# Attention: both transposes of a group's first two units before its value product

## What is computed

```
B, S, D = 8, 512, 512; N_HEAD = 16; HEAD_DIM = 32
q = (x @ Wq + bq), k = (x @ Wk + bk), v = (x @ Wv + bv)      # split in 16 heads of 32
scores = einsum('bhqd,bhkd->bhqk', q / sqrt(HEAD_DIM), k) + attention_bias
scores = where(src_mask, -inf, scores)
probs  = softmax(scores, axis=-1)
ctx    = einsum('bhqk,bhkd->bhqd', probs, v)
x      = x + (ctx @ Wo + bo)
```

## Time and profile before

| | |
|---|---|
| median of 3 executions | 2872.56 us (2868.95 to 2876.88) |
| the profiled execution | 2875.56 us, its span 2873.8 us |
| TensorE busy in the span | 2659.9 us, 93% |
| VectorE, GpSimd, ScalarE busy | 1771.7 us (62%), 1026.4 us (36%), 951.0 us (33%) |
| attention, steady part | 280 to 1195 us |
| transposes of probabilities, L1021 | 2048, 313.6 us busy |

### The profile page before, as it was taken

How to read it: one execution, slowest core, us unless ns; L and a number is a source line. 1 busy time by engine, 2 the same in 40 slices (tenths; PEclk the granted TensorE clock), 3 DMA queues, 4 the chain that set the end, 5 groups by cost and what they waited for, 6 DMA issues and landing times. The chain is left out here.

```text
span 2873.8 us, 48156 instructions
## 1 busy us (share of the span) xinstructions
PE 2659.9 (93%) x17072; PEld 2040.2 (71%) x17088; DVE 1771.7 (62%) x3500; ACT 951.0 (33%) x2032; POOL 1026.4 (36%) x741
## 2 busy tenths in 40 slices
PE   6975999999999999699999999996999999999997
PEld 2434777777777777477888888885777777777775
DVE  8965777777777777565444444433665665566544
ACT  1114666666666666311111111111112111211212
POOL 1004787777777775531111001102332222222210
PEclk9997999999999999899999999998999999999998
DMA  4325554554545545331100000001543343233311
GB/s 156 113 82 168 166 188 144 184 170 162 189 144 183 191 140 164 114 103 45 30 1 31 30 31 1 30 15 61 165 121 103 99 120 108 93 116 117 98 46 37
DMA packets 212640, 306.13 MB, mean 107 GB/s; under 512 B 14266, under 2 KB 93178, under 8 KB 209722
## 3 DMA queue, kind: packets, MB, share of 16 engines
q1 hardware_dynamic: 210682, 299.88, 32.3%
q0 software_dynamic: 1728, 3.16, 0.5%
HBM read 268.94 MB, written 34.05 MB: 105 GB/s over the span
## 5 line engine op out<-in xcount | busy, mean ns | idle before, releaser
L783 POOL TENSOR_TENSOR at_bias<-at_bias,at_mask 128x1024 f32<-128x1024 f32 x224 | 480.0, 2147 | 248.0 <-DMA at_bias<-in_fside_Bx16xSxS 246.7
L1148 DVE CUSTOM_DVE_ANT_0 at_bias<-at_bias,at_bank_score 128x512 f32<-128x512 f32 x512 | 337.7, 680 | 183.2 <-PE at_bank_score L1014 137.8
L875 ACT ACTIVATE at_y<-at_bias,at_nmax 128x512 f32<-128x512 f32 x512 | 366.5, 717 | 20.3 <-DVE at_nmax L1148 20.3
L1542 POOL TENSOR_SCALAR expert_WH<-expert_stage 128x1024 fp32r<-128x1024 f32 x128 | 164.3, 1284 | 516.4 <-PE expert_bank_out L98 315.9
L1021 PE MATMUL at_bank_probT<-at_ident,at_y 128*128 128x128 f32 x2048 | 313.6, 280 | 6.6 <-ACT at_y L875 6.6
L1876 DVE CAST ff_gH<-ff_g 128x512 fp32r<-128x512 f32 x128 | 70.0, 547 | 387.1 <-ACT ff_g L1615 386.8
L1021 PEld LDWEIGHTS at_bank_probT<-at_ident,at_y 128*128 128x128 f32 x2048 | 228.6, 141 | 94.7 <-issue 66.2
L1615 ACT ACTIVATE expert_g<-expert_bank_hid,expert_b1c 128x512 f32<-128x512 f32 x128 | 88.3, 690 | 623.7 <-PE expert_bank_hid L98 623.7
L1615 ACT ACTIVATE ff_g<-ff_bank_hid,ff_b1c 128x512 f32<-128x512 f32 x128 | 88.2, 689 | 610.1 <-PE ff_bank_hid L98 610.1
L883 ACT ACTIVATE at_probT<-at_bank_probT 128x512 f32<-128x512 f32 x256 | 153.0, 598 | 272.0 <-PE at_bank_probT L1021 159.7
L1876 DVE CAST expert_gH<-expert_g 128x512 fp32r<-128x512 f32 x128 | 68.5, 535 | 259.7 <-ACT expert_g L1615 259.7
(11 more groups left out here) (327 smaller groups left out, 5657.8 us busy)
## 6 DMA issues: line engine op xcount, KB each, us to landing
at_bias<-in_fside_Bx16xSxS SPq DMA_DIRECT2D x256, 512.0 KB, 3.5
expert_stage<-in_L_cond_Wi SPq DMA_DIRECT2D x128, 256.0 KB, 2.9
expert_stage<-in_L_cond_Wo SPq DMA_DIRECT2D x128, 256.0 KB, 3.0
st_f<-in_x SPq DMA_DIRECT2D x8, 1024.0 KB, 7.0
x_after_layer<-st_y SPq DMA_DIRECT2D x8, 1024.0 KB, 4.8
at_x<-x_after_layer SPq DMA_DIRECT2D x32, 256.0 KB, 4.6
x_after_attention<-at_x SPq DMA_DIRECT2D x32, 256.0 KB, 2.3
ff_x<-x_after_attention SPq DMA_DIRECT2D x32, 256.0 KB, 4.0
```

Source lines behind the costliest of these rows:

```text
L783: pool.tensor_tensor(bias[i % NB][:, :, :], bias[i % NB][:, :, :], mask[:, i // 2 % R, :].unsqueeze(1).to_broadcast([P, 2, S]), ALU.add).t ...
L875: act.activation(prob[u % 2][:, :], bias[u // 2 % NB][:, u % 2, :], ACT.Exp, scale=-1.0, bias=nmax[:, u % 4:u % 4 + 1], accum_out=sums[:, ...
L1148: dve.tensor_tensor_reduce(t, t, pS[u % HC][:, :], -1.0, 3.0e38, ALU.add, ALU.min, nmax[:, u % 4:u % 4 + 1]).then_inc(s_max, 1)
L1542: pool.tensor_scalar(WH[:, f, :], stage[f % 2][:, :], 1.0, 0.0, ALU.mult, ALU.add).then_inc(s_wh, 1)
```

## The change

In TensorE's loop over the units, the transposes of the second unit of a group (u mod 4 = 1) no longer stand at their own place, behind the value product of u mod 4 = 0, but directly behind the first unit's, in front of the value product. The waits go with them. The third and fourth units' transposes stay. No other engine's code is touched.

```
@@ -1069,8 +1069,10 @@
                         if nxt and u in (42, 46, 50):
                             pe.wait_ge(s_xl, (n + 1) * C + {42: 1, 46: 3, 50: 4}[u])
                         scores(n, (u + 2) // HC)
-                    if cur:
+                    if cur and u % HC != 1:
                         transpose_probs(n, u)
+                    if cur and u % HC == 0:
+                        transpose_probs(n, u + 1)
                     if u % HC == 0 and (prev or u > 4) and (cur or u <= 4):
                         values(n, u, cur)
                     if it == 2 and cur and (prev or c > 0):
```

## The result

The changed kernel takes **2926.76 us** (median of 4, 2923.69 to 2928.83) against 2874.72 before (median of 4): a ratio of **1.0188, 95% interval 1.0176 to 1.0200**, some 54 us more by the ratio. The forecast was 2929 in 2904 to 2948. The profiled execution has a span of 2924.5 us where it was 2873.8: 50.7 more.

The account below looks back on a forecast made before the run. TensorE was taken to set attention's pace. Terms 34.0 + 2.8 + 6.7 + 3.7 + 7.3 + 2 = 56.5 us took the profiled 2875.56 to 2932, a median of 2929 us; range 2904 to 2948.

Parts of the forecast that it names:

- The return path: Value product through ScalarE's even copy, exponential and context copy to next scores: 2.81 us, no longer hidden; 0.27 a group, 34.0 us.
- P directly behind V: Projections straight after the value product on TensorE: any gain or larger gap lies inside the 2.81 us path, not counted.
- The faster rival: Projections need no gap after the value product, scores don't wait for the context copy: 0.20 a group, 2847 us; chance 0.04.
- T1's wait for exp(u1): Second unit's transposes, now before the value product, wait for their exponential: 0 to 0.28 us ordinarily, more at u = 28, 32.
- u = 48: Value product at u = 0 mod 16: second transposes wait for their exponential, 0.28 us; 6.7 us over 24 groups.
- The five groups without projections: One in first batch, four at end, TensorE already idle: about 2 us over the 0.27 each, an estimate.
- u = 24: Value product at u = 8 mod 16: exponential there in time, no wait, so only the 0.27 us.
- u = 28: In 7 batches second transposes wait for an exponential ending late: 0.52 us over the 0.27, 3.7 us in all.
- u = 32: In 7 batches ScalarE has no gap, the exponential comes 0.39 later: 1.04 us each, 7.3 us in all.
- The return path alone (2907): Rival: exponentials come early enough everywhere, so only the longer path to the scores costs, 34 us; chance 0.08.
- ScalarE falling behind everywhere: Rival: no ScalarE gap after the context copy, some 94 groups wait 0.17 more, 16 us on top, 2945 us; chance 0.08.
- No change: Rival: the value product would have been waiting anyway for VectorE's sums of the scores, 2873 us; chance 0.06.

Follow-up runs that it names:

- The two edits that shorten the path: Changed kernel with ScalarE's context copy ahead of the next exponential: 2896.07 us, ratio 1.0070; changed kernel with three buffers of transposed probabilities: 2894.18 us, ratio 1.0059.
- the run with u = 24 alone: Kernel before, with the two units' transposes paired only in the group whose value product stands at u = 24 (8 groups): 2872.18 us, one execution.

## Why the prediction was right

The time, its sign and its mechanism came out; two terms of the sum did not. The distance between successive value products, after less before, was worked out from the starts of L1037 in both traces (means of the first seven batches; the last batch has other groups). A distance holds the cost of a late V and the gain of the 0.17 us by which S now follows V sooner.

| V at u | predicted | measured |
|---|---|---|
| 8, 12, 40, 44, 56, 60 | 0.27 | 0.26 to 0.33 |
| 0, 16, 48 | 0.55 | 0.53, 0.56, 0.26 |
| 4, 20, 36, 52 | 0.36 | 0.36 to 0.39 |
| 24 | 0.27 | 1.19 |
| 28 | 1.27 | -0.12 (0.52 in the first batch) |
| 32 | 0.84 | 0.74 |

**The return path: right in each number.** V after T0 0.97, S after V 2.82 (2.81), even copy at V + 1.21, 0.14 from the context copy to S. The term was 34.0 us. The two edits that shorten the path should leave 0.03 a group, so take away 30. In the traces they take 28 and 33 us off the time from the first to the last value product of attention; by the ratios it is 34 and 37, with some 7 us of uncertainty each.

**P directly behind V: right to leave out.** No row showed it. It keeps the gap of 0.20 that T1 had: V to P is 1.01. The faster rival had needed it to vanish.

**T1's wait for exp(u1): right but for u = 48.** At u = 0, 4, 16, 20, 36 and 52 as worked out, to 0.03. At u = 12 and 60 it isn't zero but 0.04: the read comes some hundredths late. At u = 48 of the full batches it is zero, not 0.28, which is 2 us less: four transposes of the next batch's rows (L960, 0.44 us) stand ahead of T0 there and give the exponential time. The five groups without projections cost some 2 us in all over the 0.27 each, as estimated.

**u = 24: the step that failed.** The prediction let T1 wait for the exponential alone, and put u = 24 with u = 8 at nothing. In seven groups, those of u = 24 in every batch but the last, it waits for the bank (and once more, for 0.2 us, in the last batch):

```profile
676.73 0.68 DVE L1109 BATCH_NORM_STATS2 at_stats<-at_x 128x6 f32<-128x512 f32 x1
676.81 0.60 PE L1021 MATMUL at_bank_probT<-at_ident,at_y 128*128 128x128 f32 x4
676.88 0.18 ACT L875 ACTIVATION_READ_ACCUMULATOR at_y<-at_bias,at_nmax 128x1 f32 x1
...
677.34 0.67 DVE L1157 COPY at_probT<-at_bank_probT 128x512 f32<-128x512 f32 x1
...
678.16 0.63 PE L1021 MATMUL at_bank_probT<-at_ident,at_y 128*128 128x128 f32 x4 [0.74 <-DVE at_probT L1157]
```

exp(u1) is over at 677.06, but the odd copy of u = 23 starts only at 677.34, behind VectorE's row statistics, and T1 waits 0.74 us until it has freed bank pT[1]. T1 in front of V has two waits, and where VectorE carries the statistics the second one comes last. In the kernel before V's 1.01 us covered it. It cost 0.93 us in 7 batches, 6.5 us.

**u = 28: the second mis-sized term.** The forecast took over the kernel before's VectorE, where the subtraction L1116 takes 1.76 us and exp(u1) is late by that. After, its time is

```profile
683.71 0.17 DVE L1118 TENSOR_SCALAR at_mneg<-at_mv 128x4 f32<-128x4 f32 x1
```

0.17 us. GpSimd's mask addition in the two kernels, first before, then after:

```profile
894.12 2.15 POOL L783 TENSOR_TENSOR at_bias<-at_bias,at_mask 128x1024 f32<-128x1024 f32 x1
```

```profile
681.13 2.14 POOL L783 TENSOR_TENSOR at_bias<-at_bias,at_mask 128x1024 f32<-128x1024 f32 x1
```

Before, 894.12 + 2.15 = 896.27 and the subtraction ends at 896.29; after, 681.13 + 2.14 = 683.27, 0.44 before it starts. The group is later by then, the mask addition is out of the way, and 1.4 us a batch come back against the forecast: 10 us. The prediction had named this row as its uncertainty but put it at 6 us either way.

**u = 32: right.** TensorE's timeline of u = 20 to 32:

```profile
915.88 1.08 PE L1037 MATMUL at_bank_score<-at_probT,at_v 128*32 128x128 f32 x32
...
924.25 1.08 PE L1037 MATMUL at_bank_score<-at_probT,at_v 128*32 128x128 f32 x32
...
931.62 1.08 PE L1037 MATMUL at_bank_score<-at_probT,at_v 128*32 128x128 f32 x32
...
937.74 0.60 PE L1021 MATMUL at_bank_probT<-at_ident,at_y 128*128 128x128 f32 x4
939.05 0.66 PE L1021 MATMUL at_bank_probT<-at_ident,at_y 128*128 128x128 f32 x4 [0.71 <-ACT at_y L875]
939.64 1.08 PE L1037 MATMUL at_bank_score<-at_probT,at_v 128*32 128x128 f32 x32
```

T1 starts 1.31 behind T0 (1.42 forecast) and V 0.59 behind that.

The sum: 56.5, plus 6.5 for u = 24, less 10 for u = 28 and 2 for u = 48, is 51; 50.7 in the span and 52 between the medians were measured. The two failed terms have opposite signs, and that the total is closer than its parts is luck. In the kernel they are tied: the run with u = 24 alone shows that the delay there is what moves the subtraction out from under the mask addition, and the run with the statistics moved, which takes the first wait away, gets nothing for it.

**The rivals.** The return path alone (2907) falls: with the path cut the kernel still loses 17 to 20 us. ScalarE falling behind everywhere falls: the classes at u = 4 and 8 are as forecast. No change and faster fall with the result.

**What the profile was to show.** The wait before the scores, the even copy's larger wait, V to S of 2.82 and T0 to V of 0.97 came. Two readings were put wrongly: the wait for L891 is named in 55 places and not in over 100, since most are too short to be given a releaser, and stands as 22.7 us of idle time in the row of L1014; and TensorE's busy time in attention did not stay but rose from 898.97 to 920.38 us, though its instructions are the same. Matmuls' ends are modelled and overlap, so that part of the lost time is booked as busy: in the group above the last projection's record ends at 736.99, and only 0.15 of the 0.22 us is booked as idle.

## What to carry to other kernels

An engine that is busy all the time can still stand on a path through other engines that is hidden by a fraction of a microsecond; before an instruction is moved in front of another, follow who is released by the one that is now later, through each in-order queue, back to the first instruction that the busy engine needs, and compare that with the busy engine's own work between the two. Of the instruction that is moved forward, list all of its semaphores and not only the one that last ended its wait: the place it had may have covered several. If two pieces are to stand together, put the one that others wait for first.

## What was not expected of the hardware

VectorE's 128 x 4 subtraction of SBUF data takes 0.17 us alone. Where it met GpSimd's f32 addition of 128 x 1024 it took up to 1.81 us in the kernel before, and ended 0.02 to 0.03 us behind the end of that addition in each of seven batches (896.29 and 896.27 in the one above). Not everything is held: a sum of scores, with one operand from PSUM, took its usual 0.68 us inside such an addition (729.00, the addition from 728.29 to 730.44), and so did four small aggregations from SBUF to SBUF (L1115, 0.38 us at 683.03 in the run with the statistics moved, the addition from 682.48; 0.37 without one). The Trainium skill (SBUF — State Buffer, SBUF: two separate sides) says that VectorE and GpSimd share a pair of ports, and that a VectorE instruction of certain forms and one of GpSimd lock it against each other for a whole instruction. The trace agrees with the lock; which form the subtraction has, no run here shows.

In the changed kernel a TensorE instruction that had been waiting started 0.05 us behind the end of ScalarE's accumulator read and 0.14 to 0.15 us behind the end of a copy out of PSUM, ScalarE's or VectorE's, each to within 0.01 us over the whole run; and T to V takes 0.58 to 0.59 after a wait for the read and 0.56 after one for the odd copy, 0.53 otherwise. Sums of this kind can be made to hundredths of a microsecond, as long as no term is missing.
